# A mixture-of-experts tower on one core: four experts' first layers to a cycle, relu by halves, and a new order on every engine

## The chip, the cores and the metric

The kernel runs on one core of a Trainium2 chip. The metric is the device time of one execution, in microseconds (us); the profile adds the span from the first to the last instruction that it recorded.

## The reference

```
h = patches(x) @ tok_W.T + tok_b                      # 16 images of 28 x 28 patches, D = 64
hid: for t in 0..15: hid_t = tanh(ln(h)_t @ W_ih.T + b_ih + b_hh + hid_(t-1) @ W_hh.T)
h = h + hid                                            # the scan runs over the 16 images
x2 = ln(h)
logits = x2 @ gate_w + gate_b; top 2 of 16 experts, softmax of the two values
moe = sum over the 2 chosen e of weight * (relu(x2 @ w1[e] + b1[e]) @ w2[e] + b2[e])
out = h + ln(x2 + moe) * gamma + beta
```

The recurrence makes the images sequential: the state of image s is needed for that of s + 1. The kernel calls an image a step (STEPS = 16). A step has 784 tokens, held as 7 tiles of 112, or with the features on the partitions as 128 x 784 in two halves of 392. All 16 experts are computed for every token, and gates that are zero for 14 of them weight the results.

## The kernel before

Five engines each run a list of instructions written out by hand, with semaphores between them; no planner orders anything. `body(t)` is the part of such a list for step t. It holds the experts of step t, and between them pieces for other steps: gates of t + 1, recurrent cell of t + 2, embedding of t + 3, closing layer norm of t - 1.

TensorE (PE). `first_layer(t, u)` (L911) is expert u's first layer: for each half of the tokens two matmuls (w1hi, w1lo) into `pZ[u % 2]`, a buffer of two banks of which there are two. `second_layer(t, q)` (L928) is experts 2q and 2q + 1 side by side into `pO`, again by halves. The order is two first layers, one second layer (of the pair before), eight times a step. Between them stand the small groups: `x2_turn` (L880, the expert input of t + 1 transposed), `embed_turn` (L843), `recur` (L853), `hidden_turn` (L863, state of t + 2), `gates_turn` (L892), `sum_turn` (L942, the experts' sum of t - 1), `embed_in` (L830, embedding of t + 3).

ScalarE (ACT). `relu(t, u)` (L503) takes a whole 128x784 `pZ` buffer into one of four `hexp`. First layer n + 2 waits for relu n, since they share a buffer. Copies and squares stand between relus: `keep_xt`, `keep_h1`, `keep_xn1t`, `new_hidden`, `keep_gt`, `square_h1` (L444), `square_h2` (L488), `close_norm` (L450, seven instructions).

VectorE (DVE). `product(t, q)` (L679, two halves) multiplies a second layer with the gates that `spread` holds for each token; `add` (L695) sums the products. Between them are the layer norms and the top-2 search. `add_state` (L597) makes `h2` of step t + 2.

GpSimd (POOL). `add_beta(s)` (L379, needs the fetched `h2c`), the second addition to `h2b` (L382), `bias_h1(t + 3)` (L372), three `rstd` (L366), and `close_out` (L387, L392).

SyncE (SP) issues every DMA of the loop, in this order in `body(t)`: `load_x(t + 4)` (L263), `fetch_h2(t - 1)` (L274: h2 comes back from DRAM as `h2c`), `keep_h2(t + 2)` (L268: h2 goes to DRAM, once `add_state` is done), `spread_gates(t + 1)` (L283 stores the gates, L295 reads them back broadcast, eight DMAs of 392 KB), `store(t - 1)` (L300). In the loop of before, `square_h1(t + 3)` stands after relu 13, and `h1_biased`, for which it waits, is counted up by `bias_h1(t + 3)`.

## Time and profile before

| | |
|---|---|
| median of 3 runs (lowest to highest) | 511.25 us (511.07 to 513.22) |
| the profiled execution: time, span | 511.07 us, 509.0 us |
| busy share of the span: PE, DVE, ACT, POOL | 97%, 88%, 67%, 36% |
| mean granted clock of TensorE | 0.992 |
| DMA engines, mean busy share of the main queue | 58.6% |

Time and span differ by 2.1 us, which lie outside the recorded instructions. A row of the timeline gives start and duration in us, engine, line and operation, destination <- source, the number of instructions merged in it, and in brackets the idle time before it with what ended it. SPq rows are the issuing of a DMA, not its transfer.

### The profile page before, as it was taken

The page shows a single profiled execution, that of the slowest core. Times are in us where ns is not written, and L with a number is a line of the kernel's source. Part 1 is how long each engine was busy: PE and PEld are TensorE (multiplying, and loading weights), DVE is VectorE, ACT ScalarE, POOL GpSimd, SP SyncE. Part 2 cuts the span into 40 slices and gives each one's busy share as a digit, 9 for nine tenths or more (in the row PEclk, how much of TensorE's full clock was granted, in tenths as well). Part 3 has the DMA queues.
Part 4 walks back from the last instruction along what each step waited for, and adds up shares of the span by engine and source line. Part 5 has one row for each costly group of instructions (what it writes and reads, how often), then busy time and mean ns, then how long its engine had stood idle before and what let it go on. Part 6 is the DMA issues. An engine that isn't in the chain of part 4 may idle for free.

```text
span 509.0 us, 8784 instructions
## 1 busy us (share of the span) xinstructions
PE 492.6 (97%) x2982; PEld 322.7 (63%) x2982; DVE 448.2 (88%) x881; ACT 342.9 (67%) x586; POOL 184.1 (36%) x137
## 2 busy tenths in 40 slices
PE   8889999999999999999999999999999999999993
PEld 5565666666667666666666666666666666666652
DVE  1678888989989898998989999999989899999775
ACT  1556766859576785867678586766858676665652
POOL 3220304436161542726144352505345362222133
PEclk9989999999999999999999999999999999999998
DMA  6229292938549292866729294483918476582911
GB/s 141 80 72 221 64 217 68 223 96 189 139 96 216 72 220 64 178 147 131 180 53 221 80 206 121 111 202 91 232 30 192 119 154 143 122 190 56 223 36 32
DMA packets 31067, 69.04 MB, mean 136 GB/s; under 512 B 6720, under 2 KB 10800, under 8 KB 30896
## 3 DMA queue, kind: packets, MB, share of 16 engines
q1 hardware_dynamic: 31024, 68.49, 58.6%
q8 instruction: 24, 0.39, 0.3%
q14 instruction: 19, 0.16, 0.1%
HBM read 60.39 MB, written 8.08 MB: 135 GB/s over the span
## 4 chain that ended last, share of the span: by engine, by line
PE 88%; DVE 3%; DMA 2%; issue 2%; SPq 1%; POOL 1%; ACT 1%; POOLq 0%; DVEq 0%; ACTq 0%
PE pZ L911 38%; PE pO L928 35%; PE pA L863 2%; PE pA L830 2%; PE pA L942 2%; PE pA L853 2%; PE pA L880 2%; DMA gbias<-gate_b 1%; PE pB L892 1%; PE pA L843 1%; PE pB L942 1%; PE pB L880 1%; PE pA L854 1%; POOL inv_std L366 1%; DMA spread<-gates_dram 1%
## 5 line engine op out<-in xcount | busy, mean ns | idle before, releaser
L503 ACT ACTIVATE hexp<-pZ,b1c 128x784 f32<-128x784 f32 x256 | 221.4, 911 | 108.7 <-PE pZ L911 108.7
L928 PE MATMUL pO<-hexp,w2s 128*64 128x392 f32 x1024 | 198.4, 504 | 0.5 <-ACT hexp L503 0.3
L911 PE MATMUL pZ<-xt,w1hi 128*128 128x392 f32 x512 | 188.8, 369 | 0.0
L679 DVE SCALAR_TENSOR_TENSOR prod<-pO,b2c,spread 128x392 f32<-128x392 f32 x256 | 150.0, 621 | 30.1 <-PE pO L928 27.9
L911 PE MATMUL pZ<-xt,w1lo 128*128 128x392 f32 x512 | 174.5, 341 | 0.0
L911 PEld LDWEIGHTS pZ<-xt,w1hi 128*128 128x128 f32 x512 | 96.6, 189 | 46.1 <-issue 19.6
L366 POOL TENSOR_TENSOR inv_std<-var,nhalf 112x7 f32<-112x7 f32 x48 | 81.5, 1705 | 105.2 <-DVE var L569 105.2
L928 PEld LDWEIGHTS pO<-hexp,w2s 128*64 128x64 f32 x1024 | 69.5, 136 | 75.6 <-issue 63.0
L695 DVE TENSOR_TENSOR acc<-acc,prod 128x784 f32<-128x784 f32 x111 | 111.7, 1006 | 0.1
L911 PEld LDWEIGHTS pZ<-xt,w1lo 128*128 128x128 f32 x512 | 97.0, 189 | 0.0
L379 POOL TENSOR_TENSOR h2b<-h2c,bet 112x448 f32<-112x448 f32 x15 | 17.0, 1134 | 162.5 <-DMA h2c<-h_dram 162.5
L372 POOL TENSOR_TENSOR h<-h,tokb 112x567 f32<-112x567 f32 x13 | 22.9, 1761 | 38.3 <-ACT h L423 38.3
L569 DVE TENSOR_REDUCE var<-sq 112x7 f32<-112x455 f32 x48 | 29.8, 620 | 4.5 <-ACT sq L444 2.2
L450 ACT ACTIVATE yn<-cen,inv_std 112x64 f32<-112x64 f32 x105 | 26.8, 335 | 4.5 <-POOL inv_std L366 4.5
L387 POOL TENSOR_TENSOR yn<-yn,gam 112x448 f32<-112x448 f32 x15 | 20.7, 1379 | 11.1 <-ACT yn L450 11.1
L392 POOL TENSOR_TENSOR yo<-yn,h2b 112x448 f32<-112x448 f32 x15 | 21.7, 1446 | 1.2
L580 DVE TENSOR_TENSOR xn<-h,inv_std 112x448 f32<-112x448 f32 x16 | 19.3, 1208 | 1.5 <-POOL inv_std L366 1.5
L863 PEld LDWEIGHTS pA<-fold,state 64*112 64x112 f32 x128 | 13.9, 176 | 9.7 <-issue 9.0
L830 PEld LDWEIGHTS pA<-tokw,xcur 64*112 64x112 f32 x112 | 12.7, 183 | 8.6 <-issue 7.9
L423 ACT ACTIVATE h<-pA 112x324 f32<-112x324 f32 x13 | 5.8, 444 | 18.3 <-PE pA L830 18.3
L382 POOL TENSOR_TENSOR h2b<-h2b,h2c 112x448 f32<-112x448 f32 x15 | 17.1, 1137 | 1.2
L863 PE MATMUL pA<-fold,state 64*112 64x81 f32 x128 | 16.3, 267 | 0.2 <-ACT state L468 0.2
(114 smaller groups left out, 501.4 us busy)
## 6 DMA issues: line engine op xcount, KB each, us to landing
spread<-gates_dram SPq DMA_DIRECT2D x126, 392.0 KB, 9.2
h_dram<-h SPq DMA_DIRECT2D x16, 248.1 KB, 2.4
h2c<-h_dram SPq DMA_DIRECT2D x16, 248.1 KB, 8.8
out<-yo SPq DMA_DIRECT2D x15, 196.0 KB, 9.2
xcur<-x_in SPq DMA_DIRECT2D x16, 112.0 KB, 7.9
xcur<-x_in SPq DMA_DIRECT2D x16, 84.0 KB, 8.7
w1f<-w SPq DMA_DIRECT2D x2, 512.0 KB, 5.8
spread<-gates_dram SPq DMA_DIRECT2D x4, 196.0 KB, 3.8
```

The source lines that it names most:

```text
L366: nc.gpsimd.tensor_tensor(inv_std[:, lane, :], var[:, lane, :], nhalf[:, :], ALU.pow)\
L372: nc.gpsimd.tensor_tensor(h1[par][:, :, :], h1[par][:, :, :], over_tiles(tokb[:, :], W), ALU.add)\
L392: nc.gpsimd.tensor_tensor(yo[:, :, :], yn[:, :, :], h2b[:, :, :], ALU.add).then_inc(CLOSE.sem, 1)
L450: last = nc.scalar.activation(yn[:, i, :], cen[:, i, :], ACT.Copy, scale=inv_std[:, 2, i:i + 1])
L503: nc.scalar.activation(hexp[u % RING][:, :].rearrange("p (b c) -> p b c", b=2), halves(pZ[u % 2]), ACT.Relu, bias=b1c[:, u:u + 1]).then_in ...
L569: nc.vector.tensor_reduce(var[:, lane, :], sq[:, lane, :, :], X, ALU.add).then_inc(chain.sem, 1)
L679: nc.vector.scalar_tensor_tensor(out=prod[q % RING][:, b * HALF:(b + 1) * HALF], in0=halves(pO)[:, b, :], scalar=b2c[:, q:q + 1], in1=spre ...
L695: nc.vector.tensor_tensor(acc[par][:, :], sofar, prod[q % RING][:, :], ALU.add).then_inc(summed, 1)
L830: last = nc.tensor.matmul(embedded_in(s)[i % 2][:, i // 2, :], xcur[s % 2][rows, (i // 2) * P:(i // 2 + 1) * P], tokw[rows, :], start=True ...
L863: last = nc.tensor.matmul(wide[i % 2][:, i // 2, :], state[rows, i % 2, (i // 2) * P:(i // 2 + 1) * P], fold[rows, :], start=True, stop=True)
L911: last = nc.tensor.matmul(halves(pZ[e % 2])[:, b, :], w[:, e, :], xt[par][:, b * HALF:(b + 1) * HALF], start=(k == 0), stop=(k == 1))
L928: last = nc.tensor.matmul(halves(pO)[k * D:(k + 1) * D, b, :], w2s[:, e, :], hexp[e % RING][:, b * HALF:(b + 1) * HALF], start=True, stop= ...
```

## The change

Every engine gets a new order in `body(t)` for t from 1 to 14, and lists of their own for the first and the last step.

- PE: a cycle is four experts' first layers, with one of the turns between the second and the third, then two second layers with `embed_in`, `recur` or `hidden_turn` between them (none in the fourth cycle). Step t now finishes its own last second layer, which before stood in step t + 1.
- `relu` is two instructions of 392 columns, and the waits between first layer, relu and second layer go by halves.
- The closing norm is split into CLOSE (up to rstd) and FINISH (norm, gamma, out). Its last part runs two steps after its experts, no longer one: `fetch_h2(t - 2)`, `add_beta(t - 2)`, `close_norm(t - 2)`, `close_out(t - 2)`, `store(t - 2)`.
- ACT: `square_h1(t + 3)` moves from after relu 13 to before relu 8.
- POOL: each piece waits until a given second layer of step t has begun. The order is rstd, `add_beta`, `add_mean`, `bias_h1(t + 3)`, `apply_gamma`, rstd, `close_out`, rstd.
- DVE: `add_state` stands between products 4 and 5, and the adds of the last three products of t - 1 stand in step t.
- `embed_in(t + 3)` waits for `xt_b` of t + 1, no longer for `h2` of t + 2.

```diff
-        CLOSE = Chain("close_stage", "turned center_a center square var rstd norm gamma out")
+        CLOSE = Chain("close_stage", "turned center_a center square var rstd")
+        FINISH = Chain("finish_stage", "norm gamma out")
...
             def fetch_h2(s):
 
+                if not known(s, 1):
+                    sp.wait_ge(h2b_set, 2 * s)
                 sp.wait_ge(h2_stored, 16 * s + 16)
                 sp.dma_start(h2c[:, :, :], h2_dram[bass.ds(s, 1), :, :, :].rearrange("s p i d -> (s p) i d"))\
...
             def body(t, par, experts=False, gate=False, mix=False, embed=False, close=False):
                 if embed and known(t + 4, STEPS):
                     load_x(t + 4)
-                if close:
-                    fetch_h2(t - 1)
+                if close and not known(t, 2):
+                    fetch_h2(t - 2)
                 if mix:
                     keep_h2(t + 2)
                 if gate:
                     spread_gates(t + 1, 1 - par)
+                if close and not known(t, 2):
+                    store(t - 2)
                 if known(STEPS - 1 - t, 1):
-
-                    sp.wait_ge(h2b_set, 2 * t)
+                    fetch_h2(t - 1)
                     fetch_h2(t)
-                if close:
                     store(t - 1)
...
                 pool.wait_ge(h2_loaded, 16 * s + 16)
+                if not known(s, 1):
+                    FINISH.wait(pool, s - 1, "out")
                 nc.gpsimd.tensor_tensor(h2b[:, :, :], h2c[:, :, 0:D], over_tiles(bet[:, :], D), ALU.add)\
                     .then_inc(h2b_set, 1)
+
+            def add_mean(s):
...
+            def apply_gamma(s):
+                FINISH.wait(pool, s, "norm")
+                nc.gpsimd.tensor_tensor(yn[:, :, :], yn[:, :, :], over_tiles(gam[:, :], D), ALU.mult)\
+                    .then_inc(FINISH.sem, 1)
...
+            def second_layer_begun(t, q):
+
+                pool.wait_ge(y_ready, 2 * (t * Q + q) + 1)
+
+            def last_body():
+                t = STEPS - 1
+                for s in (t - 2, t - 1):
+                    rstd(CLOSE, s, 2)
+                    add_beta(s)
+                    add_mean(s)
+                    apply_gamma(s)
+                    close_out(s)
 
             def body(t, par, experts=False, gate=False, mix=False, embed=False, close=False):
-                if close:
-                    add_beta(t - 1)
+                late = close and not known(t, 2)
+                if known(STEPS - 1 - t, 1):
+                    last_body()
+                    return
+                if late:
+                    rstd(CLOSE, t - 2, 2)
+                    second_layer_begun(t, 0)
+                    add_beta(t - 2)
+                    second_layer_begun(t, 1)
+                    add_mean(t - 2)
                 if embed:
+                    if close:
+                        second_layer_begun(t, 2)
                     bias_h1(t + 3, 1 - par)
-                if mix:
-                    rstd(MIX, t + 2, 1)
-                if close:
-                    rstd(CLOSE, t - 1, 2)
+                if late:
+                    second_layer_begun(t, 3)
+                    apply_gamma(t - 2)
                 if embed:
                     rstd(EMBED, t + 3, 0)
-                if close:
-                    close_out(t - 1)
+                if late:
+                    second_layer_begun(t, 4)
+                    close_out(t - 2)
+                if mix:
+                    rstd(MIX, t + 2, 1)
 
...
             def close_norm(s):
                 CLOSE.wait(act, s, "rstd")
+                if not known(s, 1):
+                    FINISH.wait(act, s - 1, "out")
...
             def relu(t, u):
+
                 n = t * E + u
-                act.wait_ge(z_ready, n + 1)
                 if known(n, 1):
                     act.wait_ge(experts_loaded, EXPERTS_LOADED)
-                if not known(n, RING):
-
-                    act.wait_ge(y_ready, t * E + 2 * (u // 2) - RING + 2)
-                nc.scalar.activation(hexp[u % RING][:, :].rearrange("p (b c) -> p b c", b=2),
-                                     halves(pZ[u % 2]), ACT.Relu, bias=b1c[:, u:u + 1]).then_inc(h_ready, 1)
+                for b in range(2):
+                    act.wait_ge(z_ready, 2 * n + b + 1)
+                    if not known(n, RING):
+                        act.wait_ge(y_ready, 2 * ((n - RING) // 2) + b + 1)
+                    nc.scalar.activation(hexp[u % RING][:, b * HALF:(b + 1) * HALF], halves(pZ[u % 2])[:, b, :],
+                                         ACT.Relu, bias=b1c[:, u:u + 1]).then_inc(h_ready, 1)
...
+            def last_body():
+                t = STEPS - 1
+                for u in range(0, 4):
+                    relu(t, u)
+                close_norm(t - 2)
+                for u in range(4, 8):
+                    relu(t, u)
+                square(CLOSE, t - 1, "center", 2, cen[:, :, :])
+                for u in range(8, 12):
+                    relu(t, u)
+                close_norm(t - 1)
+                for u in range(12, 16):
+                    relu(t, u)
 
             def body(t, par, experts=False, gate=False, mix=False, embed=False, close=False):
...
+                    return
+                if known(STEPS - 1 - t, 1):
+                    last_body()
+                    return
+                relu(t, 0)
+                relu(t, 1)
+                if gate:
+                    keep_xt(t + 1, 1 - par)
+                relu(t, 2)
+                relu(t, 3)
+                if not known(t, 2):
+                    close_norm(t - 2)
+                if embed:
+                    keep_h1(t + 3, 1 - par)
+                relu(t, 4)
+                relu(t, 5)
+                if mix:
+                    keep_xn1t(t + 2)
+                relu(t, 6)
+                if gate:
+                    exp_gap(t + 1)
+                relu(t, 7)
+                if mix:
+                    new_hidden(t + 2)
+                if embed:
+                    square_h1(t + 3, 1 - par)
+                relu(t, 8)
+                relu(t, 9)
+                if gate:
+                    keep_gt(t + 1)
+                relu(t, 10)
+                relu(t, 11)
+                if mix:
+                    square_h2(t + 2)
+                for u in range(12, 16):
+                    relu(t, u)
+                if mix:
+                    high_part(t + 2)
+                square(CLOSE, t - 1, "center", 2, cen[:, :, :])
 
             act.wait_ge(weights_made, 1)
...
+                g, s, a = t + 1, t + 2, t + 3
+                if known(t, 1):
+                    first_body()
+                    return
+                if known(STEPS - 1 - t, 1):
+                    last_body()
+                    return
+                if not known(t, 2):
+                    norm_var(CLOSE, t - 2, 2)
+                if mix:
+                    scale_h1(s, par)
+                if gate:
+                    bias_logits(g)
+                    find_first(g)
+                add(t - 1, 5, 1 - par)
+                product(t, 0, par)
+                add(t - 1, 6, 1 - par)
+                product(t, 1, par)
+                add(t - 1, 7, 1 - par)
+                if gate:
+                    find_second(g)
+                add(t, 0, par)
+                product(t, 2, par)
+                if gate:
+                    gate_weights(g)
+                product(t, 3, par)
+                if embed:
+                    norm_var(EMBED, a, 0)
+                add(t, 1, par)
+                add(t, 2, par)
+                add(t, 3, par)
+                product(t, 4, par)
+                if mix:
+                    add_state(s, par)
+                product(t, 5, par)
+                if mix:
+                    norm_var(MIX, s, 1)
+                add(t, 4, par)
+                close_center(t - 1)
+                if mix:
+                    norm_scale(MIX, s, 1, x2[:, :, :], h2[:, :, 0:D])
+                product(t, 6, par)
+                if mix:
+                    low_part(s)
+                product(t, 7, par)
...
                     pe.wait_ge(h1_kept, 2 * 1 + 2)
                 if known(n, 2) and not known(n, 1):
                     pe.wait_ge(h1_kept, 2 * 2 + 2)
-                if not known(n, 2):
-                    pe.wait_ge(h_ready, n - 1)
                 for b in range(2):
+                    if not known(n, 2):
+                        pe.wait_ge(h_ready, 2 * (n - 2) + b + 1)
                     for k, w in enumerate((w1hi, w1lo)):
                         last = nc.tensor.matmul(halves(pZ[e % 2])[:, b, :], w[:, e, :],
                                                 xt[par][:, b * HALF:(b + 1) * HALF], start=(k == 0), stop=(k == 1))
-                last.then_inc(z_ready, 1)
+                    last.then_inc(z_ready, 1)
 
             def second_layer(t, q):
 
                 n = t * Q + q
-                pe.wait_ge(h_ready, 2 * n + 2)
                 if known(n, 1):
                     pe.wait_ge(w2_centred, 1)
                     pe.wait_ge(b2_centred, 1)
                     GATE.wait(pe, 0, "gt")
                 for b in range(2):
+                    pe.wait_ge(h_ready, 2 * (2 * n + 1) + b + 1)
                     if not known(n, 1):
                         pe.wait_ge(p_ready, 2 * n - 1 + b)
                     for k in range(2):
...
+                if known(t, 1):
+                    first_body()
+                    return
+                if known(STEPS - 1 - t, 1):
+                    last_body()
+                    return
+                first_layers(t, 0, par)
+                if gate:
+                    x2_turn(t + 1)
+                first_layers(t, 2, par)
+                second_layer(t, 0)
+                if embed:
+                    embed_in(t + 3)
+                second_layer(t, 1)
+                first_layers(t, 4, par)
+                if mix:
+                    embed_turn(t + 2, embed)
+                first_layers(t, 6, par)
+                second_layer(t, 2)
+                if mix:
+                    recur(t + 2)
+                second_layer(t, 3)
+                first_layers(t, 8, par)
+                if gate:
+                    gates_turn(t + 1, embed)
+                first_layers(t, 10, par)
+                second_layer(t, 4)
+                if mix:
+                    hidden_turn(t + 2)
+                second_layer(t, 5)
+                first_layers(t, 12, par)
+                sum_turn(t - 1, 1 - par, gate, mix)
+                first_layers(t, 14, par)
+                second_layer(t, 6)
+                second_layer(t, 7)
```

## Rows read from the trace of the kernel before

**Rows 1.** The page: busy time, share of the span and instructions of each engine.
```profile
PE 492.6 (97%) x2982; PEld 322.7 (63%) x2982; DVE 448.2 (88%) x881; ACT 342.9 (67%) x586; POOL 184.1 (36%) x137
```

**Rows 2.** Windows over one step: length; busy us and instructions of PE, PEld, DVE, ACT, POOL; clock.
```profile
231.53:261.03 29.50, 29.50 (x186) 19.46 (x183) 27.38 (x56) 21.30 (x37) 11.66 (x8) 1.00 0.63 143
```

**Rows 3.** Waits, all engines: us in total, times, the longest in us.
```profile
POOL h2b L379 <- DMA h2c<-h_dram: 162.5, 15, 17.6
```

**Rows 4.** Timeline of PE around one second layer.
```profile
235.76 0.34 PE L911 MATMUL pZ<-xt,w1hi 128*128 128x392 f32 x1
235.94 0.34 PE L911 MATMUL pZ<-xt,w1lo 128*128 128x392 f32 x1
236.21 1.54 PE L928 MATMUL pO<-hexp,w2s 128*64 128x392 f32 x8
237.68 0.44 PE L911 MATMUL pZ<-xt,w1hi 128*128 128x392 f32 x1
237.96 0.34 PE L911 MATMUL pZ<-xt,w1lo 128*128 128x392 f32 x1
```

**Rows 5.** Timeline of PE at the end, two second layers in succession.
```profile
494.06 1.54 PE L928 MATMUL pO<-hexp,w2s 128*64 128x392 f32 x8
495.85 0.55 PE L928 MATMUL pO<-hexp,w2s 128*64 128x392 f32 x2 [0.26 <-DVE prod L679]
```

**Rows 6.** Timeline of SP: DMA issues of a little more than a step.
```profile
230.63 1.23 SPq L283 DMA_DIRECT2D gates_dram<-gt  x2
233.05 5.18 SPq L295 DMA_DIRECT2D spread<-gates_dram  x8
...
244.38 0.60 SPq L274 DMA_DIRECT2D h2c<-h_dram  x1
254.20 0.31 SPq L268 DMA_DIRECT2D h_dram<-h  x1
260.11 1.23 SPq L283 DMA_DIRECT2D gates_dram<-gt  x2
```

**Rows 7.** Windows of the transfers; the last two columns are DMA share and GB/s.
```profile
235.00:237.00 2.00, 2.00 (x14) 1.37 (x14) 2.00 (x4) 1.56 (x3) 1.04 (x1) 1.00 1.04 257
...
253.00:255.00 2.00, 2.00 (x12) 1.47 (x13) 1.93 (x6) 1.21 (x2) 1.47 (x2) 1.00 0.00 0
```

**Rows 8.** Tile h2c, all 16 fetches.
```profile
DMA to landing us min/median/max: 2.7/8.8/13.0
```

**Rows 9.** Timeline of POOL.
```profile
253.45 1.09 POOL L379 TENSOR_TENSOR h2b<-h2c,bet 112x448 f32<-112x448 f32 x1 [10.64 <-DMA h2c<-h_dram]
254.62 0.95 POOL L382 TENSOR_TENSOR h2b<-h2b,h2c 112x448 f32<-112x448 f32 x1
257.69 1.82 POOL L372 TENSOR_TENSOR h<-h,tokb 112x567 f32<-112x567 f32 x1 [2.13 <-ACT h L423]
...
283.34 1.08 POOL L379 TENSOR_TENSOR h2b<-h2c,bet 112x448 f32<-112x448 f32 x1 [9.86 <-DMA h2c<-h_dram]
```

**Rows 10.** Timeline of ACT, two squares of 448 columns.
```profile
234.12 0.57 ACT L435 ACTIVATE sq<-cen 112x448 f32<-112x448 f32 x1
234.59 0.58 ACT L444 ACTIVATE sq<-h 112x448 f32<-112x448 f32 x1
```

**Rows 11.** Timeline of PE, hidden_turn of one step, its first and last row.
```profile
251.82 0.32 PE L863 MATMUL pA<-fold,state 64*112 64x81 f32 x1
...
252.48 0.36 PE L863 MATMUL pA<-fold,state 64*112 64x81 f32 x2
```

**Rows 12.** Timeline of DVE, the second half of add_state of the same step.
```profile
253.77 0.40 DVE L597 TENSOR_TENSOR h<-pB,h 112x243 f32<-112x243 f32 x1
```

**Rows 13.** Windows near the start, where PE waits; the clock is the column before the last two.
```profile
27.00:30.00 3.00, 1.57 (x12) 1.12 (x12) 2.83 (x13) 1.16 (x4) 0.00 (x0) 0.95 0.00 0
30.00:33.00 3.00, 3.00 (x10) 2.55 (x12) 2.35 (x3) 1.89 (x4) 0.00 (x0) 0.50 0.08 17
```

More of the change, by code:

```diff
@@ L298, in store @@
             def store(s):
-                CLOSE.wait(sp, s, "out")
+                FINISH.wait(sp, s, "out")
                 sp.dma_start(out[bass.ds(s, 1), :, :, :].rearrange("s p i d -> (s p) i d"), yo[:, :, :])\
@@ L403, in body @@
-                if embed:
-                    rstd(EMBED, t + 3, 0)
-                if close:
-                    close_out(t - 1)
             rstd(EMBED, 0, 0)
@@ new lines, in relu, with first_body @@
+                for b in range(2):
[4 more added lines that the diff above has]
+                                         ACT.Relu, bias=b1c[:, u:u + 1]).then_inc(h_ready, 1)
+            def first_body():
+                relu(0, 2)
+                relu(0, 3)
+                relu(0, 4)
+                keep_xn1t(2)
+                relu(0, 5)
+                high_part(1)
+                new_hidden(2)
+                relu(0, 6)
+                keep_xt(1, 1)
+                relu(0, 7)
+                exp_gap(1)
+                keep_h1(3, 1)
+                relu(0, 8)
+                relu(0, 9)
+                keep_gt(1)
+                square_h1(3, 1)
+                relu(0, 10)
+                relu(0, 11)
+                square_h2(2)
+                for u in range(12, 16):
+                    relu(0, u)
+                high_part(2)
@@ L559, in _ @@
             run(act, body)
-            CLOSE.wait(act, STEPS - 2, "norm")
+            FINISH.wait(act, STEPS - 2, "norm")
             LAST.wait(act, 0, "turned")
@@ L600, in close_center @@
                 CLOSE.wait(dve, s, "turned")
+                if not known(s, 1):
+                    FINISH.wait(dve, s - 1, "norm")
                 for bank, some, n in ((pA, slice(0, PAIRS), PAIRS), (pB, slice(PAIRS, TILES), TILES - PAIRS)):
@@ new lines, in first_body @@
+            def first_body():
+                product(0, 0, 0)
+                norm_scale(MIX, 1, 1, x2[:, :, :], h2[:, :, 0:D])
+                bias_logits(1)
+                find_first(1)
+                low_part(1)
+                product(0, 1, 0)
+                find_second(1)
+                add(0, 0, 0)
+                product(0, 2, 0)
+                gate_weights(1)
+                product(0, 3, 0)
+                add(0, 1, 0)
+                add(0, 2, 0)
+                norm_var(EMBED, 3, 0)
+                product(0, 4, 0)
+                add_state(2, 0)
+                product(0, 5, 0)
+                norm_var(MIX, 2, 1)
+                add(0, 3, 0)
+                add(0, 4, 0)
+                norm_scale(MIX, 2, 1, x2[:, :, :], h2[:, :, 0:D])
+                product(0, 6, 0)
+                low_part(2)
+                product(0, 7, 0)
@@ L777, in _ @@
             last = STEPS - 1
-            add(last, Q - 2, last % 2)
-            product(last, Q - 1, last % 2)
-            CLOSE.wait(dve, last - 1, "out")
+            FINISH.wait(dve, last - 1, "out")
             dve.wait_ge(h2_loaded, 16 * STEPS)
@@ L860, in hidden_turn @@
                     MIX.wait(pe, s - 1, "xt_b")
+                if not known(s, 2):
+                    GATE.wait(pe, s - 1, "gt")
                 for i in range(TILES):
@@ L886, in gates_turn @@
                 GATE.wait(pe, s, "gates")
+                if known(s, 1):
+                    pe.wait_ge(b2_centred, 1)
+                else:
+                    MIX.wait(pe, s, "xt_b")
                 if embed and not known(s, 1):
                     pe.wait_ge(h1_kept, 2 * (s + 2) + 2)
-                elif known(s, 1):
-                    pe.wait_ge(b2_centred, 1)
                 for i in range(PAIRS):
@@ L938, in sum_turn @@
                 if not known(s, 1):
-                    CLOSE.wait(pe, s - 1, "out")
+                    CLOSE.wait(pe, s - 1, "rstd")
                 for bank, first, end in ((pA, 0, PAIRS), (pB, PAIRS, TILES)):
@@ new lines, in last_body @@
+            def last_body():
+                t, par = STEPS - 1, (STEPS - 1) % 2
+                for k in range(4):
+                    first_layers(t, 4 * k, par)
+                    if k == 1:
+                        sum_turn(t - 1, 1 - par)
+                    first_layers(t, 4 * k + 2, par)
+                    second_layer(t, 2 * k)
+                    second_layer(t, 2 * k + 1)
+            def body(t, par, experts=False, gate=False, mix=False, embed=False, close=False):
+                if known(t, 1):
+                    first_body()
+                    return
[7 more added lines that the diff above has]
+                second_layer(t, 0)
+                if embed:
+                    embed_in(t + 3)
[21 more added lines that the diff above has]
+                second_layer(t, 7)
```

160 lines of the change are left out of this document (59 added, 101 removed).

## The prediction

> **What bounds the kernel now.** I read the page first: PE is busy for 97% of the span, no other engine for more than 88% [rows 1]. The windows over one step show the same without the ends: PE 29.50 of 29.50 us, DVE 27.38, ACT 21.30 [rows 2]. So a step costs what its matmuls cost, 29.5 us, and the reader is to see that no wait of another engine is paid for today. Then I read the waits. The largest is POOL's for `h2c`, 162.5 us in 15 times, up to 17.6 us each [rows 3]. It is free now, since nothing that PE needs soon stands behind it on POOL. The question is whether that holds in the new order, so I followed that transfer through the queue of SP and the windows of the DMA engines.
>
> **What PE gains.** Within a first layer the matmuls start 0.18 us apart. The last one is followed by the second layer after 0.27, and after a second layer the first pitch is 0.28 [rows 4]. So going from first to second layer and back costs at least 0.09 + 0.10 = 0.19 us. Eight such round trips a step become four, which is worth 4 x 0.19 = 0.76 us. The bounds are 0 (the groups that now stand between second layers have seams of their own) and 1.3 us: eight first-layer matmuls and a second layer take 3.08 us, of which 8 x 0.18 are pitches and, as an estimate, 1.32 the second layer without its seams, so some 0.33 a round trip at most. I take 0.76. Against it, the fourth cycle has two second layers in succession. They share `pO`, so the second waits for the first's product. The trace has that once, at the end: 1.79 us from start to start in place of 1.47, with DVE as releaser [rows 4, 5]. That gives +0.3. A step would be 29.5 - 0.76 + 0.3 = 29.0 us if nothing else waited.
>
> **Where everything would stand.** Laid end to end with those pitches (two experts 1.5 us, a second layer 1.4 to 1.5, turns 0.3 to 0.7, groups 0.75 to 0.95), the step's PE times from its first matmul are: second layers 0 and 1 at 3.7 and 6.2 us, 2 and 3 at 11.2 and 13.3, first layer 8 at 14.7, gates turn at 16.3, first layer 10 at 16.65, second layer 4 at 18.25, hidden turn at 19.7, second layers 6 and 7 at 26.0 and 27.8. `add_state` can then end at about 21.7.
>
> **The halves of relu.** An ACT instruction of 448 columns takes 0.57 us, and the next starts 0.1 us before its end [rows 10]. I take 0.50 for 392 columns and 0.41 from one to the next. In a cycle of 7.2 us four relus then take 3.3 us; with no overlap and the full 0.57 it would be 4.6, still hidden. I cost them at nothing: the cover is the rest of the cycle. DVE has the same operations as before, 27.4 of 29.0 us, so it is close but still under PE.
>
> **The step that decides: POOL and `h2c`.** In the new order POOL runs `add_beta(t - 2)`, `add_mean(t - 2)`, then `bias_h1(t + 3)`. Behind `bias_h1` waits ACT's `square_h1(t + 3)`, which moved ahead of relu 8, and first layer 10 shares relu 8's buffer. So PE's first layer 10 waits for `h2c`. When does that land? SP issues `fetch_h2(t - 2)` at the head of `body(t)`, after the eight spread DMAs of `body(t - 1)`. The transfers go in the order of issue: in the trace the fetch is issued at 244.38 and lands only when POOL starts at 253.45, although one fetch landed in 2.7 us; the DMA engines are saturated meanwhile and idle right after [rows 6, 7, 8, 9]. From the issue of the gates' store to POOL's start, 230.63 to 253.45 is 22.8 us, and 260.11 to 283.34 is 23.2 [rows 6, 9]: 23.0. Fetching earlier in SP's list does not help, since what is ahead in the queue is the same 3.1 MB. The Trainium skill says the same of the queue ("DMA: Bandwidth & Descriptors", section "Queues, rings and completion order"): SP owns one row of rings and each DMA engine consumes its descriptors in ring order. By that rule the fetch cannot pass the spread, which agrees with the rows.
>
> And when are the gates stored? In SP's list `keep_h2(t + 2)` stands ahead, and it waits for `add_state(t + 2)`, at 21.7. Before, that was already past when the gates came (254.20 against 260.11) [rows 6]. Now the gates' store is at about 22.1, POOL's start at 22.1 + 23.0 = 45.1, which is 16.1 us into the next step of 29.0. The first layer 10 that stands behind it wants to start at 16.65.
>
> The chain from POOL's start at `h2c` onward, called 0:
> - beta to the second addition 1.17, that one 0.95, `bias_h1` 1.82: 3.95 [rows 9];
> - `square_h1`, 0.47 to the start of the next, half a relu of 0.50, and two hand-overs of 0.08: 1.1 [rows 10], first layer 10 starts at 5.0;
> - PE now goes at the pace of the half relus (0.41): three of them, then two matmuls and the seam: 1.7, second layer 4 at 6.7;
> - second layer 1.47 [rows 4], the hidden turn to its end 1.02 and a hand-over of 0.1 [rows 11]: 9.3;
> - `add_state`, its second part ending 0.80 after its start, and SP at 254.20: 0.85 [rows 6, 12]; 10.15;
> - issue of `keep_h2`, 0.31 [rows 6]: the gates' store at 10.5;
> - 23.0 to POOL's start in the next step: 33.5.
>
> It closes on itself. So while it rules, a step takes 33.5 us and not 29.0, and PE stands still for 4.5 us ahead of first layer 10. It rules where both `late` and `embed` hold, t = 2 to 12: 11 steps.
>
> **The clock.** Near the start PE was busy 1.57 of 3 us, and the granted clock went from the upper of its two levels (2.4 GHz) to the lower (1.2) for 0.3 us of that window and all of the next 3 us [rows 13]. A pause of 4.5 us in each step is longer. Such a stretch costs at most 3.3 / 2 = 1.65 us of work, and 0 if it falls into the pause itself. I take half, 0.85 to 0.9, on the stretch from first layer 10 to the hidden turn, which is in the chain: 34.4 us a step. The Trainium skill ("TensorE: Matmul & The Clock Gate", section "HAM oscillation") tells of the same pattern, a wait in each tile that sends the clock down each time; the row at the start agrees as far as it goes.
>
> **The sum.** Against the span of 509.0 us. Eleven steps: 11 x (34.4 - 29.5) = +53.9, less 0.6 since the first of them starts from the unstretched phase. Steps 0, 1, 13 and 14: 4 x -0.5 = -2.0. Last step: -0.5, and +1.9, because `close_norm(14)` now stands before relu 12 on ACT and needs a `rstd` that stands behind all of image 13's closing on POOL, which again begins with an `h2c`. In total +52.7, a span of 561.7, and with the 2.1 us outside it 563.8: 564 us. The profiled execution (511.07) is within 0.2 us of the median, so no correction.
>
> **The rivals.**
> - *The chain rules, the clock stays up* (25%): 33.5 us a step, 11 x 0.9 less, 554 us. For it: the pause may end before the clock is taken down, and rows 13 is one case. Against: the pause there was shorter.
> - *The chain is shorter than I make it* (8%): a landing 2 us sooner, or first layer 10 later than I laid it, leaves a stall of 2 to 3 us: 31 to 32 us a step, 525 to 540 us.
> - *No chain, the gain shows* (11%): the fetch passes the spread. Issued some 2 us into the step and landing after 2.7 us as the quickest did [rows 8], it would be there at 5, and `bias_h1` would run at its place behind second layer 2. Then 15 steps of 29.0 and the last unstalled: 511 - 8 = 503 us. The point that decides: POOL must start on `h2c` by 16.65 - 5.0 = 11.6 us into the step; each us later costs one. At 12.1 the sign turns. Rows 6 to 9 speak against it.
> - *The chain is longer* (8%): the clock costs the full 1.65 and the adds 1 to 3, which now stand before product 4 beside POOL's `rstd`, delay `add_state` by up to a microsecond: 36 us a step, 575 to 585 us.
> - My forecast (the chain, with the clock falling): 48%, 558 to 572 us by itself.
>
> **How the numbers follow.** The range leaves out the gain and the better part of the short chain, and the end of the long one: 538 to 583. About 0.5% (2.5 us) is what a measurement tells from no change. Faster: the 11% of no chain and a little of the short one's far end, 0.12. Same: the stall would have to hit 0.5 us, 0.03. Slower: 0.85.
>
> **What would show it.** Right: in the waits of the new profile PE, idle in the 2% now, waits for ACT's relu some 11 times for 4 to 5 us each, before a first layer 10; ACT's `square_h1` waits for POOL's `bias_h1`, and POOL's L379 equivalent for the DMA of `h2c`; step lengths of 33 to 35 us from t = 2 to 12 and 29 around them; granted clock 0.5 after the pauses. The seams: first-layer blocks of four with one entry each, second layers 6 and 7 some 1.8 us apart. Wrong: `h2c` landing before 12 us into the step, or PE waits spread over other instructions. If the step is 33.5 with a full clock, only the clock term falls.

## The result and the profile after

The changed kernel takes 568.3 us (median of 4, 565.8 to 571.0) against 512.2 us for the kernel before: a ratio of 1.110, 95% interval 1.104 to 1.116. The forecast was 564, range 538 to 583. The profiled execution took 571.0 us with a span of 569.0, so it is one of the longer ones; before it was 511.1 and 509.0.

The page after, busy time and the slices of PE and its clock (compare [rows 1]):

```profile
PE 507.4 (89%) x2982; PEld 336.2 (59%) x2982; DVE 437.5 (77%) x881; ACT 378.4 (67%) x842; POOL 181.7 (32%) x137
...
PE   7899999699797997979979798998979979998993
...
PEclk9889999989899997999989899898999989999998
```

PE has the same 2982 matmul records and 15 us more of busy time, at a share of 89% where it was 97. The dips in the PE row come at an even distance, and the clock row dips beside them.

The windows of some steps, from one `x2_turn` to the next (columns as in [rows 2], then DMA share and GB/s):

```profile
93.94:129.68 35.74, 31.19 (x184) 20.99 (x182) 26.56 (x55) 23.53 (x54) 11.58 (x9) 0.90 0.54 121
129.68:164.24 34.56, 30.64 (x183) 20.60 (x182) 26.49 (x55) 23.52 (x54) 11.58 (x9) 0.95 0.49 116
...
440.30:474.50 34.20, 30.77 (x184) 20.27 (x182) 26.57 (x55) 23.55 (x54) 11.61 (x9) 0.95 0.55 124
64.90:93.94 29.04, 28.78 (x184) 19.64 (x182) 25.89 (x53) 21.99 (x47) 5.78 (x4) 1.00 0.54 120
474.50:503.58 29.08, 28.00 (x170) 18.98 (x169) 26.89 (x55) 22.36 (x51) 10.04 (x7) 1.00 0.55 128
```

The row from 64.90 begins in step 1, which has no fetch: 29.04 us, PE busy nearly throughout, clock 1.00. The next eleven intervals, 93.94 to 474.50, take 380.6 us together, 34.6 each, at a clock of 0.90 to 0.95. Then it is 29.08 again (28.58 in the kernel before, for that step 13). Eleven times 34.6 - 29.5 is 56 of the 60 us that the span grew.

The waits (as [rows 3]):

```profile
POOL h2b L380 <- DMA h2c<-h_dram: 136.6, 11, 13.1
...
ACT sq L474 <- POOL h L371: 47.4, 11, 5.1
PEld pZ L1058 <- ACT hexp L536: 45.7, 35, 4.5
DVE var L654 <- ACT sq L474: 45.3, 14, 4.7
...
PE pZ L1058 <- ACT hexp L536: 38.2, 11, 4.3
```

L380 is `add_beta`, L371 `bias_h1`, L474 `square_h1`, L536 `relu`, L1058 `first_layer`. The same eleven events stand there at each link: POOL waits for the fetched `h2c`, ACT's square for POOL, PE's first layer for ACT's relu. The kernel before has one such row for the weight loads, 15.9 us in 26 times, none above 0.6 us.

One step of it in order of time, one timeline with the rows of SP, POOL, ACT, PE and DVE (compare [rows 6, 9, 11, 12]):

```profile
263.44 5.27 SPq L294 DMA_DIRECT2D spread<-gates_dram  x8
...
270.62 0.53 SPq L273 DMA_DIRECT2D h2c<-h_dram  x1
...
283.22 1.08 POOL L380 TENSOR_TENSOR h2b<-h2c,bet 112x448 f32<-112x448 f32 x1 [11.99 <-DMA h2c<-h_dram]
...
284.28 0.55 PE L1039 MATMUL pB<-ident,gates 112*32 112x112 f32 x4
...
285.35 1.30 POOL L371 TENSOR_TENSOR h<-h,tokb 112x567 f32<-112x567 f32 x1
...
286.68 0.58 ACT L474 ACTIVATE sq<-h 112x448 f32<-112x448 f32 x1 [3.94 <-POOL h L371]
...
287.29 2.02 ACT L536 ACTIVATE hexp<-pZ,b1c 128x392 f32<-128x392 f32 x4
...
287.93 0.45 PE L1058 MATMUL pZ<-xt,w1hi 128*128 128x392 f32 x1 [3.10 <-ACT hexp L536]
...
290.49 2.36 PE L1075 MATMUL pO<-hexp,w2s 128*64 128x392 f32 x8
...
292.78 0.32 PE L1008 MATMUL pA<-fold,state 64*112 64x81 f32 x1
...
294.24 0.40 DVE L682 TENSOR_TENSOR h<-pB,h 112x243 f32<-112x243 f32 x1
...
294.67 0.31 SPq L265 DMA_DIRECT2D h_dram<-h  x1
...
295.02 1.23 SPq L282 DMA_DIRECT2D gates_dram<-gt  x2
```

The reader sees the loop close. The fetch is issued 7.2 us after the first spread and lands 12.6 us after its own issue. POOL starts at once, PE stands from the gates turn (284.28) to 287.93, and the next gates' store is issued at 295.02, 11.8 us after POOL's start. The spread that follows it carries the next fetch behind it. In the same stretch the second layer takes 2.29 us to the next matmul where it took 1.47: the clock.

```profile
285.00:287.00 2.00, 0.00 (x0) 0.00 (x0) 0.00 (x0) 0.32 (x1) 2.00 (x3) 1.00 0.00 0
287.00:289.00 2.00, 1.07 (x5) 0.71 (x5) 1.60 (x3) 1.98 (x5) 1.73 (x2) 0.95 0.01 4
289.00:291.00 2.00, 2.00 (x7) 1.34 (x8) 1.86 (x2) 2.00 (x5) 1.15 (x1) 0.50 0.00 0
291.00:293.00 2.00, 2.00 (x12) 0.69 (x10) 0.72 (x2) 0.57 (x2) 0.84 (x1) 0.70 0.00 0
```

In these windows PE does nothing for 2 us, and the granted clock stands at half all through the window from 289 and into the next, so the low stretch lies almost wholly on work and not in the pause: PE goes on at 287.93, and by these shares the clock falls at about 288.8. The clock record has it so in nine of the eleven steps: it falls between 0.2 us before PE goes on and 1.2 us after. In the other two it falls 0.7 and 2.1 us before, and the low stretch is twice as long; these are the longest steps, 36.0 and 35.7 us, with a mean clock of 0.91 and 0.90.

### The profile page after: what moved, and what is told of

It reads as the page before. It is cut to its first block and busy times, and to the rows that moved or that the text cites. A ratio compares the mean times of both kernels' runs of the same rounds, so it can differ in the third digit from the quotient of the medians.

```text
span 569.0 us, 9526 instructions
## 1 busy us (share of the span) xinstructions
PE 507.4 (89%) x2982; PEld 336.2 (59%) x2982; DVE 437.5 (77%) x881; ACT 378.4 (67%) x842; POOL 181.7 (32%) x137
## 5 line engine op out<-in xcount | busy, mean ns | idle before, releaser
L536 ACT ACTIVATE hexp<-pZ,b1c 128x392 f32<-128x392 f32 x512 | 259.1, 590 | 62.5 <-PE pZ L1058 62.1
L1058 PE MATMUL pZ<-xt,w1hi 128*128 128x392 f32 x512 | 195.9, 383 | 38.4 <-ACT hexp L536 38.2
L1075 PE MATMUL pO<-hexp,w2s 128*64 128x392 f32 x1024 | 206.7, 520 | 8.5 <-DVE prod L766 8.5
L1058 PE MATMUL pZ<-xt,w1lo 128*128 128x392 f32 x512 | 180.8, 353 | 0.0
L1058 PEld LDWEIGHTS pZ<-xt,w1hi 128*128 128x128 f32 x512 | 100.2, 196 | 85.3 <-ACT hexp L536 45.7
L365 POOL TENSOR_TENSOR inv_std<-var,nhalf 112x7 f32<-112x7 f32 x48 | 94.3, 1965 | 166.4 <-DVE var L654 163.5
L1058 PEld LDWEIGHTS pZ<-xt,w1lo 128*128 128x128 f32 x512 | 101.2, 198 | 0.0
L380 POOL TENSOR_TENSOR h2b<-h2c,bet 112x448 f32<-112x448 f32 x15 | 16.3, 1088 | 165.4 <-DMA h2c<-h_dram 136.6
L474 ACT ACTIVATE sq<-h 112x448 f32<-112x448 f32 x16 | 9.3, 582 | 50.3 <-POOL h L371 47.4
L520 ACT ACTIVATE sq<-h 112x448 f32<-112x448 f32 x16 | 9.4, 585 | 43.1 <-DVE h L682 43.1
L397 POOL TENSOR_TENSOR yo<-yn,h2b 112x448 f32<-112x448 f32 x15 | 18.2, 1214 | 22.7 <-PE pO L1075 22.3
L371 POOL TENSOR_TENSOR h<-h,tokb 112x567 f32<-112x567 f32 x13 | 16.9, 1298 | 25.1 <-PE pO L1075 15.1
## 6 DMA issues: line engine op xcount, KB each, us to landing
h2c<-h_dram SPq DMA_DIRECT2D x16, 248.1 KB, 12.3
out<-yo SPq DMA_DIRECT2D x15, 196.0 KB, 12.6
xcur<-x_in SPq DMA_DIRECT2D x16, 112.0 KB, 11.9
xcur<-x_in SPq DMA_DIRECT2D x16, 84.0 KB, 12.1
w1f<-w SPq DMA_DIRECT2D x2, 512.0 KB, 5.8
```

Source lines behind the costliest of these rows:

```text
L365: nc.gpsimd.tensor_tensor(inv_std[:, lane, :], var[:, lane, :], nhalf[:, :], ALU.pow)\
L371: nc.gpsimd.tensor_tensor(h1[par][:, :, :], h1[par][:, :, :], over_tiles(tokb[:, :], W), ALU.add)\
L397: nc.gpsimd.tensor_tensor(yo[:, :, :], yn[:, :, :], h2b[:, :, :], ALU.add).then_inc(FINISH.sem, 1)
L536: nc.scalar.activation(hexp[u % RING][:, b * HALF:(b + 1) * HALF], halves(pZ[u % 2])[:, b, :], ACT.Relu, bias=b1c[:, u:u + 1]).then_inc(h_ ...
L1058: last = nc.tensor.matmul(halves(pZ[e % 2])[:, b, :], w[:, e, :], xt[par][:, b * HALF:(b + 1) * HALF], start=(k == 0), stop=(k == 1))
L1075: last = nc.tensor.matmul(halves(pO)[k * D:(k + 1) * D, b, :], w2s[:, e, :], hexp[e % RING][:, b * HALF:(b + 1) * HALF], start=True, stop= ...
```

## The experiments

Twelve kernels ran. All of them compute the whole result but for what two of them add, which is said there. The kernel before ran beside each group, at 512.0 to 512.5 us.

### Where the chain can be cut, and where it can't

**bias_h1 ahead of add_beta.** POOL's list alone:

```diff
-                    second_layer_begun(t, 0)
-                    add_beta(t - 2)
-                    second_layer_begun(t, 1)
-                    add_mean(t - 2)
                 if embed:
                     if close:
                         second_layer_begun(t, 2)
                     bias_h1(t + 3, 1 - par)
                 if late:
+                    add_beta(t - 2)
+                    add_mean(t - 2)
                     second_layer_begun(t, 3)
```

> Changed kernel, POOL alone reordered: bias_h1(t + 3) runs before add_beta(t - 2), still once second layer 2 has begun; the whole computation is done. Theory (the chain through h2c, add_beta, bias_h1, square_h1, relu 8, first layer 10): nothing that PE needs stands behind h2c any more, the pauses before first layer 10 vanish and the eleven long steps fall from 34.6 us to the 29.04 of body 1: 568 - 11 x 5.56 = 507 us, faster than the kernel before (512). Rival (ACT cannot keep up with relu by halves in the new order, or POOL's pacing waits hold things up): the pauses stay in large part, 545 us or more.

Measured: 519.0 us, 1.014 of before (1.011 to 1.017). The pauses before first layer 10 are gone, and it takes 49 us less than the changed kernel; the transfer is as late as ever. The steps take 29.9 us, not 29.04. The rest is one wait, in each step, ahead of second layer 5: 1.68 to 2.09 us from the start of the hidden turn to it, where 0.94 is usual. POOL's work on `h2c` now runs beside DVE's adds, and both become longer. The three adds ahead of product 4 take 3.12 us in all eleven steps of the changed kernel and 4.39 to 4.79 here in ten of the eleven; POOL's second addition to `h2b` takes 0.95 us in the changed kernel and 1.56 to 2.01 here in the same ten. In the eleventh POOL's additions come earlier, and two of DVE's small operations on the gate weights take 1.1 and 1.0 us in place of 0.3. The adds of one step of the changed kernel, then a pair of this one:

```profile
287.84 3.12 DVE L782 TENSOR_TENSOR acc<-acc,prod 128x784 f32<-128x784 f32 x3
...
227.46 4.44 DVE L780 TENSOR_TENSOR acc<-acc,prod 128x784 f32<-128x784 f32 x3
...
227.59 1.65 POOL L385 TENSOR_TENSOR h2b<-h2b,h2c 112x448 f32<-112x448 f32 x1
```

```profile
212.85:242.70 29.85, 28.86 (x184) 19.73 (x182) 27.43 (x55) 23.54 (x54) 13.12 (x9) 1.00 0.63 147
```

DVE is busy 27.43 us of such a step, 26.5 in the changed kernel. So the mechanism held, and the size was 12 us off.

**The fetch ahead of the spread.** SP's list alone:

```diff
-                if close and not known(t, 2):
-                    fetch_h2(t - 2)
                 if mix:
                     keep_h2(t + 2)
+                if close and not known(STEPS - 1 - t, 1):
+                    fetch_h2(t - 1)
                 if gate:
                     spread_gates(t + 1, 1 - par)
```

> Changed kernel, SP alone reordered: the fetch of h2c for step t - 1 is issued in body t after keep_h2 and before the eight spread DMAs, so it is ahead of them in the queue; POOL's order stays; the whole computation is done. Theory (h2c is late because it queues behind the spread): it lands some 3 us after its issue and is there when the next step begins, no pause, 29.0 to 29.2 us a step, 505 to 508 us. Rival (h2c's transfer is slow by itself, or the order of issue does not matter): landing still 12 us or so into the step, 560 us or more. Rival (the gates, now behind it, come late): pauses of DVE before product 0, 1 us a step, 515 to 520.

Measured: 511.5 us, 0.999 of before (0.997 to 1.001). The fetches:

```profile
DMA to landing us min/median/max: 2.7/3.3/8.2
```

Their median is 3.3 us from issue to landing; in the changed kernel it is 12.3, with the same bytes and the same POOL, ACT, DVE and PE lists. So the place in the queue makes the lateness. The steps take 29.34 us. The 0.3 above 29.04 is again a wait for product 4 ahead of second layer 5: 1.24 us from the start of the hidden turn to it in place of 0.94. The rule that was cited ahead of the run, in the Trainium skill "DMA: Bandwidth & Descriptors" (section "Queues, rings and completion order"), agrees with this: the descriptors are consumed in ring order.

**Without the pacing waits.** `second_layer_begun` does nothing.

> Changed kernel without POOL's waits for the begin of second layers; the whole computation is done. Theory (POOL waits for the transfer, not for PE): eleven pauses as before, 564 to 572 us. Rival (the pacing waits make bias_h1 late): the pauses go, 510 us or less.

Measured: 564.7 us (2 runs), eleven pauses. POOL waits for the transfer, not for PE. It takes 3.6 us less (564.0 to 565.5 against 565.8 to 571.0). Part of that is seen in the profile: in two of its eleven steps the clock stays at the upper level, and these take 32.2 us where the others take 33.4 to 36.1. Whether the pacing has to do with it was not tested. One of the two:

```profile
128.25:160.48 32.23, 29.41 (x184) 19.49 (x182) 26.47 (x55) 23.57 (x54) 12.27 (x9) 1.00 0.53 120
```

**One more DMA ahead of the fetch.** The added transfer goes to a tile that no one reads:

```diff
+                if not known(s, 1):
+                    sp.wait_ge(more_in, 16 * (s - 1))
+                    sp.dma_start(more[0:D, :, :], src[:, q0:q0 + n, :].to_broadcast([D, n, TOK])).then_inc(more_in, 16)
```

> Changed kernel with one more broadcast DMA of 392 KB (a ninth) behind the eight spread DMAs and ahead of the fetch, into a tile that no one reads; all else as it was. Theory (a queue in order of issue, and the fetch at its end on the chain that closes on itself): at the 215 GB/s of the spread it takes 1.9 us, each of the eleven long steps grows by that and the others by nothing: 568 + 21 = 589 us. Rival (the pause comes from something else on POOL or ACT): 568 us.

Measured: 591.1 us (2 runs), 22.8 more. The median landing of the fetch goes from 12.3 to 13.6 us:

```profile
DMA to landing us min/median/max: 2.7/13.6/15.0
```

The eleven steps take 36.3 us and not 34.6, the steps around them 29.07 and 28.78 (29.04 and 29.08 in the changed kernel). From the gates' store to POOL's start it takes 24.3 us in the mean for 22.7, and 12.1 back to the store for 11.9. Nothing but the queue was touched: it is the dose that shows the queue on the chain.

**Square, then variance, then POOL's order late.** These three move the other end of the chain. First `square_h1` alone, behind relu 11:

> Changed kernel with ACT's square_h1(t + 3) behind relu 11 and no longer before relu 8; the whole computation is done. Theory: first layer 10 is free, but DVE's norm_var(EMBED), which needs the square and stands before adds 1 to 3 and product 4, holds the same chain: PE now pauses before second layer 5, which needs product 4, and the chain by way of product 4 and add_state to the gates' store is about as long: 33 to 34.5 us a step, 553 to 566 us. Rival (only the relu was held): 507 to 512 us.

Measured: 583.4 us (2 runs), slower than the changed kernel. The pause did move to second layer 5, which waits for product 4. But even step 1, in which nothing is fetched, takes 35.3 us. So this kernel has a pause of its own: DVE's `norm_var` waits for a square that comes after relu 11, and the products wait behind it. It shows that DVE is a second lock; of `h2c` it shows nothing, and my number for it had left that out.

Then DVE's `norm_var(EMBED)` behind product 5 as well:

> As the one before, and DVE's norm_var(EMBED) behind product 5; the whole computation is done. Theory: the late h2c now holds nothing that PE or the gates' store needs, no pauses, 29.3 to 29.8 us a step, 510 to 516 us. If POOL's own lateness is what matters (rstd(MIX) behind it): pauses at x2_turn, over 525 us.

Measured: 564.7 us, 1.104 of before. It missed: the second case of the expectation came true. A pause stands between second layers 6 and 7:

```profile
289.75 1.54 PE L1075 MATMUL pO<-hexp,w2s 128*64 128x392 f32 x8
293.88 0.92 PE L1075 MATMUL pO<-hexp,w2s 128*64 128x392 f32 x2 [2.59 <-DVE prod L766]
```

DVE's scaling ahead of product 6 waits for POOL's `rstd(MIX)`, which now stands behind `rstd(EMBED)` and `close_out`; in that stretch POOL itself waits for DVE's variance and not for `h2c`. So the third kernel puts `rstd(EMBED)` behind `rstd(MIX)`, and exchanges the two variances on DVE:

```diff
-                if embed:
-                    rstd(EMBED, t + 3, 0)
                 if late:
                     second_layer_begun(t, 4)
                     close_out(t - 2)
                 if mix:
                     rstd(MIX, t + 2, 1)
+                if embed:
+                    rstd(EMBED, t + 3, 0)
```

> As the kernel with square and norm_var late (564.7 us), and now POOL runs close_out and rstd(MIX) ahead of rstd(EMBED), DVE norm_var(MIX) ahead of norm_var(EMBED); the whole computation is done. The former run showed its pause between second layers 6 and 7, where DVE waits for rstd(MIX) behind 3 us of POOL work. Theory (the late h2c is harmless once nothing near PE stands behind it): that pause goes, what stays is up to 0.8 us at the gates turn, where POOL's late additions stretch DVE: 29.4 to 30.2 us a step, 511 to 521 us. If h2c is still on the chain: over 530 us.

Measured: 515.7 us, 1.009 of before (1.006 to 1.012). The transfer is untouched:

```profile
DMA to landing us min/median/max: 2.6/12.4/13.1
```

12.4 us to landing, as in the changed kernel, and steps of 29.2 to 30.2 us. So a late `h2c` makes no pause of several us once nothing near PE stands behind it. It is not free: five of the eleven steps wait about 1 us ahead of second layer 5 (not at the gates turn, as expected), where the three adds take 5.2 to 5.4 us beside POOL's work on `h2c` and `bias_h1`, and the kernel takes 4 us more than the one with the fetch first. This run moved three things at once, so it does not tell what each is worth.

### The clock

Sixteen 128x512 matmuls of zeros into `pA`, which is idle between `new_hidden` and the hidden turn, stand before first layer 10 in steps 2 to 12; no one reads them.

```diff
+                if mix and embed and not known(t, 2):
+                    STATE.wait(pe, t + 2, "hid")
+                    for _ in range(16):
+                        nc.tensor.matmul(pA[:, :], busy[:, 0:128], busy[:, :], start=True, stop=True)
                 first_layers(t, 10, par)
```

> Changed kernel with sixteen extra 128x512 matmuls of zeros into the idle bank pA between gates turn and first layer 10 in steps 2 to 12 (about 3.5 us of work that no one reads). Theory (the pause takes the clock down, and the stretch at the lower clock lies in the chain): the granted clock stays at the upper level, a step falls from 34.6 to about 33.7, in all 10 us less, 558 us. If the clock costs nothing: 568 as now. If the extra matmuls end after relu 8: longer by what they overhang.

Measured: 554.8 us, 13.6 less. The timeline of PE where the pause was:

```profile
240.13 3.92 PE L1175 MATMUL pA<-busy 128*128 128x512 f32 x16
243.89 0.34 PE L1058 MATMUL pZ<-xt,w1hi 128*128 128x392 f32 x1
...
245.55 1.54 PE L1075 MATMUL pO<-hexp,w2s 128*64 128x392 f32 x8
247.01 0.32 PE L1008 MATMUL pA<-fold,state 64*112 64x81 f32 x1
```

The second layer takes 1.46 us again to the next matmul, not 2.29, and the mean clock is 0.994 where it was 0.952. From POOL's start to the next gates' store it takes 10.4 us in eight of eleven steps (10.4 to 10.8 in all), against 11.4 to 12.9 in the changed kernel. Adding work shortened the kernel by 2.4%, since PE would have stood still. The zeros outlast the pause a little: the first half of relu 8 ends at 243.51 and first layer 10 starts at 243.89, so the 10.4 us may hold up to 0.3 us of waiting for them, and the clock alone may cost a little more than the difference.

### The parts of the change by themselves

**relu by halves alone**, in the order of before, with the waits by halves.

> Kernel before, with relu in two instructions of 392 columns and the waits by halves alone, in the old order; the whole computation is done. Theory (hidden behind PE): 512 us, within 0.5%, with ACT's busy share up by 7 points. Rival (ACT's longer relus hold PE up, 0.19 us a step and expert): slower, 515 to 520 us.

Measured: 513.6 us, 1.003 of before (1.002 to 1.005). A step takes 29.64 us for 29.48. ACT is busy 2.3 us more in a step (compare [rows 2]), and PE waits a little for relus (one step):

```profile
271.40:301.00 29.60, 29.47 (x184) 19.44 (x182) 27.68 (x55) 23.64 (x55) 12.00 (x9) 1.00 0.65 151
```

**The best versions.** On the kernel with the fetch first, add 3 goes behind product 5:

```diff
                 add(t, 2, par)
-                add(t, 3, par)
                 product(t, 4, par)
                 if mix:
                     add_state(s, par)
                 product(t, 5, par)
+                add(t, 3, par)
```

> The kernel with the fetch ahead of the spread (511.5 us), and DVE's add 3 moved from before product 4 to behind product 5; the whole computation is done. There the steps take 29.34 us, with 0.3 us of waiting between hidden turn and second layer 5, since product 4 starts late behind three adds. Theory: that wait goes, 29.04 us a step, 508 us, faster than the kernel before by 0.5 to 1%. If DVE is full: the wait turns up at another product, 511.

Measured: 509.7 us, 0.994 of before (0.992 to 0.996), the fastest of all. The steps take 29.15 us, eleven of the twelve from step 1 to 12 (one takes 29.48); two of them:

```profile
239.60:268.78 29.18, 28.82 (x184) 19.69 (x182) 26.99 (x55) 23.67 (x54) 11.92 (x9) 1.00 0.60 139
268.78:297.90 29.12, 28.73 (x183) 19.59 (x182) 27.00 (x55) 23.63 (x54) 11.89 (x9) 1.00 0.65 148
```

Then `sum_turn` between second layers 6 and 7:

> As the one before, and sum_turn moved to between second layers 6 and 7 to fill the 0.43 us that second layer 7 waits for product 6; close_center stands behind low_part, product 0 ahead of add 5 of t - 1; the whole computation is done. Theory: 0.43 less for the wait, up to 0.3 more for two seams: 28.9 us a step, 506 us. Rival (the center now delays product 7 and with it DVE's start of the next step): 0.6 us more a step, 515 us.

Measured: 512.4 us, 1.000 of before (0.998 to 1.002). The steps take 29.15 us as well: 0.98 us for the group of transposes between two second layers, where they took 0.68 between first layers, and four first layers in succession cost 3.29 us. The step ahead of the last two takes 29.6 us where it took 28.7. No gain.

Last, pairs again in the last two steps of PE:

> The kernel with fetch first and add 3 late (509.7 us), with PE's order in the last two steps again two first layers to one second layer, as in the kernel before; the whole computation is done. In those two steps no group stands between second layers, and a cycle of four measured 6.55 us there against 2 x 3.09 in the order before. Theory (second layers in succession wait 0.43 us for the product, and four first layers in succession wait 0.1 for relu, which is more than the saved seam of 0.2): 8 x 0.37 less some, 2.0 to 2.9 us less than 509.7, 507 us. If the cycle of four is as good there: no change.

Measured: 512.4 us, 1.001 of before (0.999 to 1.003): a miss. The pairs themselves ran at 3.09 us as thought, but the gates turn of step 14 now waits 1.8 us for the gate weights, and second layer 7 starts 2.8 us after 6 in that step and 3.3 in the last, where 1.9 is usual in this kernel. The order of PE can't go back alone; DVE's would have to follow. The profiled executions of this kernel and of the one before it also reach step 1 some 1.2 us later than the fastest version does, with the same instructions up to there, so 1.2 us of the 4.3 and 3.7 us between the profiled spans (511.8 and 511.2 against 507.5) is not the edit.

## Why the prediction was right, point by point

- **The deciding step.** PE pauses before first layer 10 eleven times, for the reasons given, in steps 2 to 12. Shown: the waits name each link; cutting at SP's queue, at POOL's order or (with three moves) at the ACT and DVE end each takes the pauses away, and a longer queue makes them longer. PE's idle time there is 2.5 to 4.3 us, 3.5 in the mean, where the forecast had 4.5; the rest of the 34.6 is slower work behind it.
- **"Fetching earlier in SP's list does not help" was wrong.** It holds only for a place behind the spread. Issued late in the step before, ahead of the spread, the fetch lands after 3.3 us and the kernel takes 511.5 us. The rest of the forecast does not hang on this sentence.
- **The chain's length.** 23.0 us from gates' store to POOL's start: 22.7 in the mean of eleven (21.7 to 23.5). 10.5 back to the store without the clock: 10.4 with the extra matmuls. That the second figure fits so well is in part luck, since two terms were off and cancelled: `bias_h1` took 1.30 us and not 1.82 (3.4 in place of 3.95 for POOL's three), and from its end to first layer 10 it took 1.6 us in that run for 1.1, of which up to 0.3 are the zeros' own. From there to second layer 4 it took 1.66, the 1.7 forecast.
- **The clock.** Right in kind, too small. I took 0.85 to 0.9 us a step, half of the bound. Without the extra matmuls the chain's second part is 11.9 us, with them 10.4 to 10.8: 1.4, and over the run 13.6 us for 9.9 forecast. The step that was mis-sized is "I take half": in most steps the fall came as PE went on, so that the low stretch lay on work, as in the windows above. The median lies 4.3 us above the forecast, and the profiled span 7.3 (569.0 against 561.7). Of the 7.3, 3.0 lie in the eleven steps, where a step with the zeros takes 33.2 us for the 33.5 forecast without the clock, and the clock takes 15 us between the two profiled executions for the 9.9; 4.3 lie outside them.
- **What PE gains.** 29.04 us for a step without waits, forecast 29.0. The seams' 0.76 and the wait of second layer 7 came out together; singly, that wait is 0.43 (the two start 1.80 us apart; a second layer with `recur` behind it takes 1.37) for 0.3.
- **relu by halves cost nothing:** nearly. They take 590 ns each, not 500, and cost 0.16 us a step in the old order.
- **DVE close, but under PE:** true only with POOL early. With the long pauses cut, product 4 behind three adds costs 0.2 to 1.2 us a step: 0.3 where the adds take 3.1 us, up to 1.2 where POOL runs beside them and they take 4.4 to 5.4. That is much of why the cut kernels landed at 511 to 519 and not at 507. My rival without a chain, 503 us, had left it out and was wrong by 8 us even with its condition met. By the profile with the fetch first, about half of that lies in the eleven steps, and the rest in steps 0 and 13 and in the last two.
- **The ends.** The term +1.9 for `close_norm(14)` did not come: from `x2_turn` of step 14 to the end it is 65.4 us after and 62.8 before, and no relu waits for that norm. What is there instead are second layers in succession without groups between them, 3.27 us for a pair of them, and a wait of 1.1 us for product 4 in step 14. The first step took 0.95 us more, forecast 0.5 less. That is +3.6 for both ends against +0.4 forecast. Step 13 took 0.5 us more, where the forecast took 0.5 off: the kernel before ran it in 28.6 us, not in the 29.5 from which the gain was counted. These misses are small beside the chain.

The pieces against the profiled span: eleven steps +56.3, the tail +2.7, the first step +0.9, step 1 -0.5, step 13 +0.5, start +0.1; that is the 60.0.

## What to carry to other kernels

The transfer's lateness was set here by what is ahead of it in its queue. So when an instruction in an in-order list comes to stand behind it, ask for the whole way back: here POOL as the consumer, ACT, PE, DVE, the next store and the queue again made a loop of 34.6 us beside a step of 29. An order change that is worth 0.3 to 0.4 us a step is lost to one such wait; follow each moved instruction through all five lists before looking at the engine that bounds. If a pause of PE can't be avoided, idle matmuls in it can pay.

## What was not expected of the hardware

The granted clock falls from the upper to the lower level in or just after each of the eleven pauses (2.8 to 4.5 us from the last matmul's start to the next), and 3.9 us of matmuls of zeros keep it up. In the kernel with `bias_h1` first, a wait of about 0.7 us in each step leaves it at 1.00. The length of the pause alone does not decide: in the kernel without pacing waits two pauses of 2.8 us (steps 3 and 8) left the clock up, while 2.4 and 2.7 us in two others brought it down.

Additions on DVE and on POOL that run side by side are longer: three adds of 128x784 take 3.12 us in the changed kernel, where none of POOL's operations of 448 or 567 columns runs beside them, and 4.4 to 5.4 us in the two kernels where two or more do, and POOL's second addition to `h2b` goes from 0.95 to between 1.5 and 2.0 us.

And the relu of 392 columns takes 590 ns where a copy of 448 takes 559, so its two halves add 0.27 us over one of 784 (911 ns) in duration. Of the 4.3 us a step that this makes for 16 relus, 2.3 are seen in ACT's busy time, since successive instructions overlap, and 0.16 in the step.
